# A decoder layer on one core: the next head's first two key projections spread over five places inside the triangular joins

## The chip, the cores and the metric

One core of a Trainium2 chip runs the whole kernel in one launch. Its engines are TensorE (PE; its weight loads are shown apart as PEld), VectorE (DVE), ScalarE (ACT), GpSimd (POOL) and SyncE (SP), which issues the DMAs. Every engine works through its own instructions in order and they meet at semaphores. The metric is the device time of one execution in microseconds (us), the median of several runs.

## The reference

The layer adds three terms to x of shape (4, 512, 512), each on a layer-normalised input: a gated delta-rule attention with 16 heads, a cross attention against a context, and a routed low-rank feed-forward. Only the first is touched here. In short:

```python
qkv = silu(causal_conv4(x @ Wqkv))          # per head: q, k, v of 512 tokens x 128
z   = x @ Wz
q, k = l2norm(q) / sqrt(128), l2norm(k)
for t in range(512):                        # per batch and head, M is 128 x 128
    M = M * exp(g[t])
    M = M + outer(k[t], (v[t] - k[t] @ M) * beta[t])
    o[t] = q[t] @ M
out = rmsnorm(o) * norm_w * silu(z);  x = x + out @ Wout
```

## The kernel before

The 16 heads run one after another. A head treats all 4 batches together, and the 512 tokens of each in 4 chunks (`NC`) of 128. Within a chunk the recurrence is solved in closed form, which needs the inverse of a unit lower triangular 128x128 matrix for each of the 16 (chunk, batch) units. In the order of TensorE's instructions a head consists of these stages:

1. **Decays and Grams** (lines 615 to 648): for each chunk the decay products, the transposes of k, and k times k.
2. **Jobs** (lines 694 to 705): the projections of this head's last queries and of z. One projection job is 12 matmuls of 512 columns (`proj`, line 562): four slices of the contraction, each as hi x hi, lo x hi and hi x lo. A job's result stands in one PSUM bank; ScalarE applies the last tap (`tap`), VectorE the other three (`conv`), ScalarE the silu. Between the jobs stand the transposes of v (line 669) and q (line 659). The transposes of q all use bank 2, and each waits until ScalarE has squared the one before it (`q_squares`, line 1100).
3. **Joins** (lines 787 to 804). Meanwhile GpSimd has inverted the 16x16 diagonal blocks (lines 1783 to 1792) and SyncE has brought them through DRAM into `t32` (line 452). The joins double the inverted blocks from 16 to 32, 64 and 128. Each is a pair of products, y and z, with a PSUM eviction between them (`keep...` on ScalarE, `join...` on VectorE). The matmuls are small: 16x16, 32x32 and 64x64 corners of the array. From 32 on each step comes once for chunks 0 and 1 (group 0) and once for chunks 2 and 3 (group 1). Products of keys and queries (`qk`, line 691) stand between them.
4. **Recursion** over the 4 chunks (lines 807 to 838), full-size matmuls again.

The projections of the next head, 7 jobs of 12 matmuls (`AHEAD`), serve as filling. `ahead(count)` issues the next `count` matmuls of this list:

```python
for m in range(part[0], min(part[0] + count, AHEAD * 3 * ND)):
    job, n = divmod(m, 3 * ND)
    if n == 0:
        job_waits(h + 1, job)
    proj(*JOBS[job], JOB_BANK[job], n, n + 1)
```

Before, the first job (key of batch 0, 12 matmuls) is issued in one piece ahead of the last job of this head, 12 more in four blocks of 7, 2, 2 and 1 in the joins (`JOIN_FILL`), and 60 in the recursion (`FILL`). The last head has no filling. All of TensorE's heads are written out; the other engines loop over the middle ones.

Of the kernel before, what the change touches and what calls it, by code (L numbers as in the profile page):

```python
# [32 lines left out]
ACT = mybir.ActivationFunctionType  # L33
# [6 lines left out]
ND = D // P  # L40
# [20 lines left out]
AHEAD = 7  # L61
JOB_BANK = [{Q_: (0, 3, 0, 3)[b], Z_: 1}.get(kind, job % 2) for job, (kind, b) in enumerate(JOBS)]

FILL = ((0, 6), (9, 9), (9, 9), (9, 9))
JOIN_FILL = (7, 2, 2, 1)
HALVES = 2
EARLY, LATE = slice(0, P // 2), slice(P // 2, P)
FRONT = [slice(2 * j * PAIR, 2 * j * PAIR + PAIR) for j in range(2)]
# [8 lines left out]
def layer(nc, x, ctxT, w_heads, w_ba, conv_w, a_log, dt_bias, norm_w, w_out, wqT, bq, wkT, bk, aT, bwT, wgT, out):  # L77
# [24 lines left out]
    ident = sb("ident", [P, P])  # L102
# [21 lines left out]
    q_sq = sb("q_sq", [P, B, NC])  # L124
# [11 lines left out]
    qT = sb("qT", [P, B, NC, P])  # L136
# [11 lines left out]
    y64 = sb("y64", [P, NC, B, P // 2])  # L148
    y1 = sb("y1", [P, 2, B, P])
    w1 = sb("w1", [P, 2, B, P])  # L150
    vv = sb("vv", [P, B, P])
# [6 lines left out]
    y32 = at(place["gt_0"][0], "y32", [P, NC, B, PAIR])  # L158
# [84 lines left out]
    def grid(i):  # L243

        return bank[i][:, :].rearrange("p (b t) -> p b t", b=B)
# [9 lines left out]
    def ktr_bank(c):  # L255

        return (2, 0, 0, 2)[c]

    sems = {}

    def sem(name):
# [18 lines left out]
    head_vecs, gt_done, decay_mm, decay_done, gam_mm, gam_done = (  # L280
        sem(n) for n in ("head_vecs", "gt_done", "decay_mm", "decay_done", "gam_mm", "gam_done"))
# [3 lines left out]
    qtr_done, qsq_done, qeps_done, vtr_done, nv_done, qk_mm, pT_done, qg_done, kg_done = (  # L285
        sem(n) for n in ("qtr_done", "qsq_done", "qeps_done", "vtr_done", "nv_done", "qk_mm", "pT_done", "qg_done", "kg_done"))
# [83 lines left out]
    with nc.Block() as block:  # L370
# [151 lines left out]
        def _(pe):  # L522
            mm, tr = nc.tensor.matmul, nc.tensor.transpose
# [89 lines left out]
            def head(h, first, more):  # L613

                for c in range(NC):
# [12 lines left out]
                    for b in range(B):  # L628
                        last = tr(grid(ktr_bank(c))[:, b, :], kT[:, b, c, :], ident[:, :])
# [11 lines left out]
                    for b in range(B):  # L641
                        last = mm(grid(5 + 2 * (c % 2))[:, b, :], kT[:, b, c, :], kT[:, b, c, :], start=True, stop=True)
# [7 lines left out]

                def q_transpose(b):
                    pe.wait_ge(silu_done, 12 * h + conv_index(Q_, b) + 1)
                    if b:
                        pe.wait_ge(qsq_done, 4 * h + b)
                    else:
                        pe.wait_ge(ktok_done, 4 * h + 4)
                        pe.wait_ge(ksq_done, 4 * h + 4)
                    for c in range(NC):
                        last = tr(grid(2)[:, c, :], qT[:, b, c, :], ident[:, :])  # L659
                    last.then_inc(qtr_done, 1)  # L660

                def v_transpose(b):
# [11 lines left out]
                def ahead(count):  # L674

                    if not more:
                        return
# [5 lines that stand above are left out]
                    part[0] += count  # L683
# [12 lines left out]
                for job in range(2 * B, NJ):  # L696
                    kind, b = JOBS[job]
                    if job == NJ - 1:
                        ahead(3 * ND)
                        q_transpose(b - 1)  # L700
                    whole_job(h, job)
                    if kind == Z_:
                        v_transpose(b)
                        if b:
                            q_transpose(b if job == NJ - 1 else b - 1)
# [28 lines left out]
                def join32_y(g):  # L734

                    pe.wait_ge(t32_done, 4 * h + 2 * g + 2)
                    if g and not more:
                        pe.wait_ge(y32_done, 2 * h + 1)
                    hold(pe, "pe")
                    for i in range(2):  # L740
                        for b in range(B):
                            for j in range(2):
                                c = 2 * g + i
                                last = mm(small(front_bank(g, j), BACK[j], i, b), nT[FRONT[j], b, c, BACK[j]],
                                          t32[FRONT[j], b, c, FRONT[j]], start=True, stop=True)
                    last.then_inc(y32_mm, 1)

                def join32_z(g):
                    pe.wait_ge(y32_done, 2 * h + g + 1)
                    if g and not more:  # L750
                        pe.wait_ge(z32_done, 2 * h + 1)
                        pe.wait_ge(z32n_done, 2 * h + 1)
                    hold(pe, "pe")
                    for i in range(2):
                        for b in range(B):
                            c = 2 * g + i
                            for j in range(2):
                                mm(small(back_bank(g, j), FRONT[j], i, b), y32[BACK[j], c, b, :], tT[BACK[j], b, c, BACK[j]],
                                   start=True, stop=True)
                            last = mm(small(back_bank(g, 0), BACK[0], i, b), tT[BACK[0], b, c, BACK[0]], y32[BACK[0], c, b, :],  # L760
                                      start=True, stop=True)
                    last.then_inc(z32_mm, 1)

                def join64_y(g):
                    pe.wait_ge(z32n_done, 2 * h + g + 1)
                    if g == 0:
                        pe.wait_ge(pT_done, 4 * h + 4)
                    hold(pe, "pe")
                    for i in range(2):
                        for b in range(B):  # L770
                            c = 2 * g + i
                            last = mm(large(half_bank(g), LATE, i, b), nT[EARLY, b, c, LATE], t32[EARLY, b, c, EARLY],  # L772
                                      start=True, stop=True)
                    last.then_inc(y64_mm, 1)

                def join64_z(g):
                    pe.wait_ge(y64_done, 2 * h + g + 1)
                    pe.wait_ge(z32_done, 2 * h + g + 1)
                    hold(pe, "pe")
                    for i in range(2):  # L780
                        for b in range(B):
                            c = 2 * g + i
                            last = mm(large(half_bank(g), EARLY, i, b), y64[LATE, c, b, :], tT[LATE, b, c, LATE],  # L783
                                      start=True, stop=True)
                    last.then_inc(z64_mm, 1)
# [1 line left out]
                qk(0)  # L787
                qk(1)
                join16_y()
                ahead(JOIN_FILL[0])  # L790
                join16_z()
                qk(2)
                qk(3)
                ahead(JOIN_FILL[1])
                join32_y(0)
                ahead(JOIN_FILL[2])
                join32_y(1)
                join32_z(0)
                ahead(JOIN_FILL[3])
                join32_z(1)  # L800
                join64_y(0)
                join64_y(1)
                join64_z(0)
                join64_z(1)


                for c in range(NC):
# [3 lines left out]
                    else:  # L811
                        pe.wait_ge(s_done, 3 * h + c)
                        pe.wait_ge(kg_done, 3 * h + c)
                        for b in range(B):
                            last = mm(grid(2)[:, b, :], kdT[:, b, c - 1, :], state[:, c % 2, b, :], start=True, stop=True)  # L815
# [4 lines left out]
                    for b in range(B):  # L820
                        last = mm(grid(3)[:, b, :], tT[:, b, c, :], nv[:, b, c, :], start=True, stop=True)  # L821
# [183 lines left out]
        def _(act):  # L1005
            fn = nc.scalar.activation
# [64 lines left out]
            def head(h, more):  # L1071
# [21 lines left out]
                def q_squares(b):  # L1093
                    act.wait_ge(qtr_done, 4 * h + b + 1)
                    if b:
                        act.wait_ge(qsq_done, 4 * h + b)
                    else:
                        act.wait_ge(ksq_done, 4 * h + 4)
                    for c in range(NC):
                        last = fn(vv[:, c, :], grid(2)[:, c, :], ACT.Square, accum_out=q_sq[:, b, c:c + 1])  # L1100
                    last.then_inc(qsq_done, 1)

                def z_silu(b):
# [67 lines left out]
                def keep32_n(g):  # L1171
                    act.wait_ge(z32_mm, 2 * h + g + 1)
                    fn(t32[BACK[0], :, 2 * g:2 * g + 2, FRONT[0]].rearrange("p b c s -> p c b s"),
                       smalls(back_bank(g, 0), BACK[0]), ACT.Copy, scale=-1.0).then_inc(z32n_done, 1)

                def keep64_y(g):
                    act.wait_ge(y64_mm, 2 * h + g + 1)
                    act.wait_ge(z64_mm, 2 * h)
                    fn(y64[LATE, 2 * g:2 * g + 2, :, :], larges(half_bank(g), LATE), ACT.Copy).then_inc(y64_done, 1)
# [15 lines left out]
                keep32_y(1)  # L1195
                keep32_n(0)
                keep32_n(1)
                if more:
                    tap(h + 1, K_, 1)
                keep64_y(0)  # L1200
                keep64_y(1)


                for c in range(NC):
# [701 lines left out]
```

## Time and profile before

| | |
|---|---|
| median of 3 runs | 2014.83 us (2008.29 to 2018.30) |
| the profiled execution | 2019.99 us, of which the span is 2018.3 |
| PE busy in the span | 1908.4 us (95%) |
| DVE, ACT, POOL busy | 1128.2, 933.0, 743.3 us |
| mean granted TensorE clock | 0.962 of full speed |
| 15 heads, from start of head 0 to start of head 15 | 1394.3 us |

A head here runs from its first decay product (line 619) to that of the next head. Where a time is given as "+43.9" it counts from that start. The profiler draws a matmul longer than it keeps the engine, since matmuls are pipelined; what a matmul costs is the distance between the starts of neighbours.

### The profile page before, as it was taken

What the parts mean: (1) busy time and instruction counts of PE and PEld (TensorE: products, weight loads), DVE (VectorE), ACT (ScalarE), POOL (GpSimd) and SP (SyncE); (2) the same over time, 40 slices, a digit from 0 to 9 for tenths busy, and PEclk for the clock granted to TensorE, in tenths of its full rate; (3) what the DMA queues carried; (4) which work ended last, traced back from release to release, by engine and by line L of the source; (5) the groups of instructions that cost most, each with busy time, mean ns of one, the idle gap of its engine ahead of it and who ended that gap; (6) DMA issues with size and microseconds to landing.
All of it is one profiled execution on the core that took longest, in us unless ns stands there. A gap on an engine that the chain in (4) does not pass through costs nothing.

```text
span 2018.3 us, 45513 instructions
## 1 busy us (share of the span) xinstructions
PE 1908.4 (95%) x16962; PEld 1558.9 (77%) x16962; DVE 1128.2 (56%) x2048; ACT 933.0 (46%) x2987; POOL 743.3 (37%) x1143
## 2 busy tenths in 40 slices
PE   6899999999999999999999999999997799999999
PEld 4688888888888888888888788888887565656574
DVE  6656566565657465655657574656564352524333
ACT  2556464646455555646465655546463221213121
POOL 1345363645445353636264544536361000000000
PEclk9899899999989899989999998999897899999999
DMA  3011111201021111112020111111113503121200
GB/s 117 6 33 40 25 37 28 43 22 38 22 42 29 32 40 25 34 25 44 21 43 22 38 30 35 40 24 36 25 30 145 156 21 94 42 84 52 61 23 21
DMA packets 220198, 87.12 MB, mean 43 GB/s; under 512 B 138320, under 2 KB 204240, under 8 KB 219280
## 3 DMA queue, kind: packets, MB, share of 16 engines
q1 hardware_dynamic: 220048, 84.83, 16.6%
q8 instruction: 130, 2.13, 0.4%
q14 instruction: 20, 0.16, 0.0%
HBM read 57.28 MB, written 27.53 MB: 42 GB/s over the span
## 4 chain that ended last, share of the span: by engine, by line
PE 60%; issue 21%; DVE 9%; ACT 5%; POOL 4%; DMA 1%; POOLq 0%; DVEq 0%; SPq 0%; ACTq 0%
PE bank L562 27%; PE bank L871 4%; DVE vT L1383 3%; PE bank L821 3%; PE bank L830 2%; PE bank L783 2%; PE bank L772 2%; PE bank L691 2%; PE bank L815 2%; ACT vv L1084 2%; PE bank L837 1%; PE bank L934 1%; PE bank L952 1%; PE bank L669 1%; PE bank L659 1%
## 5 line engine op out<-in xcount | busy, mean ns | idle before, releaser
L562 PE MATMUL bank<-x_hi,w_hi 128*128 128x512 f32 x1024 | 429.8, 420 | 14.7 <-DVE vT L1383 14.3
L562 PE MATMUL bank<-x_hi,w_lo 128*128 128x512 f32 x1024 | 408.9, 399 | 1.8 <-issue 1.8
L562 PE MATMUL bank<-x_lo,w_hi 128*128 128x512 f32 x1024 | 406.5, 397 | 0.0
L562 PEld LDWEIGHTS bank<-x_hi,w_hi 128*128 128x128 f32 x1024 | 196.0, 191 | 55.6 <-issue 13.4
L562 PEld LDWEIGHTS bank<-x_hi,w_lo 128*128 128x128 f32 x1024 | 195.7, 191 | 45.6 <-issue 2.2
L562 PEld LDWEIGHTS bank<-x_lo,w_hi 128*128 128x128 f32 x1024 | 196.6, 192 | 32.0 <-issue 0.6
L1383 DVE SCALAR_TENSOR_TENSOR qT<-bank,cw,qT 128x511 f32<-128x511 f32 (+2 forms) x192 | 142.1, 747 | 51.0 <-ACT qT L1033 46.5
L1848 POOL TENSOR_TENSOR rstd<-ve,mhalf 128x1 f32<-128x1 f32 x32 | 17.4, 544 | 390.2 <-DVE ve L1607 390.2
L1216 ACT ACTIVATE o_tmp<-bank 128x128 f32<-128x128 f32 x256 | 67.4, 278 | 179.0 <-PE bank L837 179.0
L1383 DVE SCALAR_TENSOR_TENSOR vT<-bank,cw,vT 128x511 f32<-128x511 f32 (+2 forms) x192 | 143.0, 745 | 8.6 <-ACT vT L1033 4.1
L1383 DVE SCALAR_TENSOR_TENSOR kT<-bank,cw,kT 128x511 f32<-128x511 f32 (+2 forms) x192 | 143.4, 747 | 5.0
L1816 POOL TENSOR_TENSOR o_rstd<-o_ms,minus_half 128x4 f32<-128x4 f32 x64 | 70.5, 1101 | 200.4 <-DVE o_ms L1525 200.4
L1805 POOL TENSOR_TENSOR qT<-qT,gam 128x512 f32<-128x512 f32 x48 | 59.9, 1275 | 182.0 <-PE bank L691 182.0
L1821 POOL TENSOR_TENSOR state<-state,gam 128x512 f32<-128x512 f32 x32 | 33.6, 1051 | 209.0 <-PE bank L837 204.7
L871 PE MATMUL bank<-wo_hi,o_hi 128*128 128x512 f32 x256 | 105.4, 412 | 0.0
L871 PE MATMUL bank<-wo_hi,o_lo 128*128 128x512 f32 x256 | 100.0, 391 | 0.0
L871 PE MATMUL bank<-wo_lo,o_hi 128*128 128x512 f32 x256 | 100.0, 391 | 0.0
L1484 DVE STREAM_TRANSPOSE tT<-t 128x512 f32<-128x512 f32 x64 | 39.9, 680 | 98.3 <-DMA t<-blkT_d 98.3
L837 PE MATMUL bank<-w,pT 128*128 128x128 f32 x512 | 92.0, 277 | 0.0
L1210 ACT ACTIVATE w<-bank 128x512 f32<-128x512 f32 x64 | 38.3, 598 | 111.1 <-PE bank L821 111.1
L1118 ACT ACTIVATE nv<-bank,k_norm 128x128 f32<-128x128 f32 x256 | 72.9, 374 | 33.0 <-PE bank L669 33.0
L1788 POOL TENSOR_TENSOR prod<-blkN,blkT 128x15 f32<-128x15 f32 (+7 forms) x240 | 65.9, 275 | 54.2 <-DMA blkN<-blkN_d 36.7
(221 smaller groups left out, 4447.3 us busy)
## 6 DMA issues: line engine op xcount, KB each, us to landing
w_raw<-in_w_heads SPq DMA_DIRECT2D x64, 256.0 KB, 2.8
o_d<-og SPq DMA_DIRECT2D x64, 256.0 KB, 2.6
o_raw<-o_d SPq DMA_DIRECT2D x16, 1024.0 KB, 6.2
x_in<-in_x SPq DMA_DIRECT2D x16, 256.0 KB, 3.6
blkN_d<-nT SPq DMA_DIRECT2D x64, 64.0 KB, 2.0
t<-blkT_d SPq DMA_DIRECT2D x64, 64.0 KB, 2.4
wo_raw<-in_w_out SPq DMA_DIRECT2D x4, 1024.0 KB, 9.5
x_res<-in_x SPq DMA_DIRECT2D x16, 256.0 KB, 2.8
```

Source lines behind the costliest of these rows:

```text
L562: last = mm(bank[bk][:, :], w[:, kind % 2, d, :], xx[:, d, b * S:(b + 1) * S], start=(n == 0), stop=(n == 3 * ND - 1))
L691: last = mm(grid(5 + 2 * (c % 2))[:, b, :], kT[:, b, c, :], qT[:, b, c, :], start=True, stop=True)
L772: last = mm(large(half_bank(g), LATE, i, b), nT[EARLY, b, c, LATE], t32[EARLY, b, c, EARLY], start=True, stop=True)
L821: last = mm(grid(3)[:, b, :], tT[:, b, c, :], nv[:, b, c, :], start=True, stop=True)
L837: last = mm(grid(4)[:, b, :], pT[:, b, c, :], w1[:, c % 2, b, :], start=(c == 0), stop=True)
L871: last = mm(bank[c % 2][:, :], o[:, c % 2, k, :], w[:, k, :], start=(n == 0), stop=(n == 3 * H - 1))
L1118: last = fn(nv[:, b, c, :], grid(6)[:, c, :], ACT.Copy, scale=k_norm[:, b, c:c + 1])
L1216: last = fn(o_tmp[:, b, :], grid(4)[:, b, :], ACT.Square, accum_out=o_sq[:, c, b:b + 1])
L1383: stt(d[:, k:S], bank[JOB_BANK[JOBS.index((kind, b))]][:, 0:S - k], cw[:, kind, TAPS - 1 - k:TAPS - k], d[:, k:S], ALU.mult, ALU.add).then ...
L1788: tt(products, blkN[:, j, j + 1:BLK].unsqueeze(2).to_broadcast([P, below, j + 1]), blkT[:, j, 0:j + 1].unsqueeze(1).to_broadcast([P, below ...
L1805: tt(qT[:, :, c, :], qT[:, :, c, :], gam[:, :, c, :], ALU.mult).then_inc(qg_done, 1)
L1816: tt(o_rstd[:, c, :], o_ms[:, c, :], minus_half[:, 0:B], ALU.pow).then_inc(orstd_done, 1)
```

## The change

The first key job is no longer issued in one piece ahead of the last job of the head. Its 12 matmuls and the 12 that were in the joins before (the second key job) now stand in the joins in five blocks: 8 before the z product of the 16-join, 5 before y of the 32-join, 5 before z of it, 3 before y of the 64-join and 3 before z of it. In the 32-join the two groups' y steps now follow each other directly, and so do their z steps. The transposes of q alternate between bank 2 and bank 4, so each waits for the squares of the one before the last. ScalarE's tap of the second key job moves behind the two evictions of the 64-join's y.

```diff
-JOIN_FILL = (7, 2, 2, 1)
+JOIN_FILL = {"z16": 8, "y32": 5, "z32": 5, "y64": 3, "z64": 3}
...
+    def qtr_bank(b):
+        return (2, 4)[b % 2]
...
                 def q_transpose(b):
                     pe.wait_ge(silu_done, 12 * h + conv_index(Q_, b) + 1)
-                    if b:
-                        pe.wait_ge(qsq_done, 4 * h + b)
+                    if b >= 2:
+                        pe.wait_ge(qsq_done, 4 * h + b - 1)
+                    elif b:
+                        pe.wait_ge(gam_done, 4 * h + 4)
...
                     if job == NJ - 1:
-                        ahead(3 * ND)
                         q_transpose(b - 1)
                     whole_job(h, job)
...
                 join16_y()
-                ahead(JOIN_FILL[0])
+                ahead(JOIN_FILL["z16"])
                 join16_z()
                 qk(2)
                 qk(3)
-                ahead(JOIN_FILL[1])
+                ahead(JOIN_FILL["y32"])
                 join32_y(0)
-                ahead(JOIN_FILL[2])
                 join32_y(1)
+                ahead(JOIN_FILL["z32"])
                 join32_z(0)
-                ahead(JOIN_FILL[3])
                 join32_z(1)
+                ahead(JOIN_FILL["y64"])
                 join64_y(0)
                 join64_y(1)
+                ahead(JOIN_FILL["z64"])
                 join64_z(0)
                 join64_z(1)
...
                 keep32_n(1)
+                keep64_y(0)
+                keep64_y(1)
                 if more:
                     tap(h + 1, K_, 1)
-                keep64_y(0)
-                keep64_y(1)
```

## Rows read from the trace of the kernel before

**Rows 1.** The page: span, and busy time of each engine.

```profile
span 2018.3 us, 45513 instructions
...
PE 1908.4 (95%) x16962; PEld 1558.9 (77%) x16962; DVE 1128.2 (56%) x2048; ACT 933.0 (46%) x2987; POOL 743.3 (37%) x1143
```

**Rows 2.** Windows, one per head: start:end, length, busy times, PEclk, DMA; heads 1, 2, 8, sum.

```profile
170.20:265.50 95.30, 92.36 (x956) 80.26 (x954) 56.82 (x97) 51.23 (x175) 44.78 (x68) 0.95 0.15 32
265.50:354.40 88.90, 87.65 (x955) 76.00 (x954) 56.67 (x96) 51.24 (x175) 44.92 (x68) 1.00 0.15 34
...
822.60:917.20 94.60, 91.51 (x954) 78.78 (x953) 56.71 (x97) 51.24 (x175) 44.81 (x68) 0.95 0.14 32
...
sum 1394.30, PE 1356.51 PEld 1176.62 DVE 850.93 ACT 768.48 POOL 671.20; mean PE 90.43 PEld 78.44 DVE 56.73 ACT 51.23 POOL 44.75
```

**Rows 3.** TensorE's waits in heads 0 to 14 together: total, times, longest.

```profile
PE bank L730 <- issue: 7.5, 13, 2.3
...
PE bank L758 <- issue: 5.2, 5, 1.4
PE bank L719 <- ACT vv L1100: 3.7, 15, 0.3
PE bank L691 <- issue: 3.7, 3, 1.8
...
PE bank L760 <- issue: 2.3, 2, 1.3
PE bank L562 <- issue: 1.8, 1, 1.8
PE bank L772 <- issue: 1.6, 2, 1.0
```

**Rows 4.** Windows late in the joins and behind them, head 1, then head 2.

```profile
224.20:227.60 3.40, 2.12 (x66) 1.69 (x66) 1.58 (x4) 1.45 (x4) 0.84 (x1) 1.00 0.00 0
227.60:237.90 10.30, 10.30 (x71) 9.60 (x70) 4.29 (x7) 2.00 (x4) 0.52 (x1) 0.50 0.09 28
...
319.50:322.90 3.40, 3.40 (x91) 3.36 (x82) 2.92 (x6) 2.25 (x4) 0.69 (x2) 1.00 0.02 5
322.90:333.20 10.30, 10.26 (x77) 9.21 (x76) 6.88 (x13) 3.55 (x12) 2.06 (x2) 1.00 0.11 27
```

**Rows 5.** The page's DMA queue that carries instructions.

```profile
q8 instruction: 130, 2.13, 0.4%
```

**Rows 6.** TensorE's timeline in head 10 (start, us, what, count, idle before).

```profile
1045.21 0.47 PE L562 MATMUL bank<-x_hi,w_hi 128*128 128x512 f32 x1
...
1048.04 0.60 PE L659 MATMUL bank<-ident,qT 128*128 128x128 f32 x4
...
1054.32 1.25 PE L719 MATMUL bank<-t,nT 16*32 16x16 f32 x128 [0.24 <-ACT vv L1100]
1055.50 0.50 PE L562 MATMUL bank<-x_hi,w_hi 128*128 128x512 f32 x1
...
1057.33 0.89 PE L730 MATMUL bank<-tT,y 32*16 32x16 f32 x88
...
1060.91 0.47 PE L562 MATMUL bank<-x_lo,w_hi 128*128 128x512 f32 x1
...
1061.58 0.69 PE L744 MATMUL bank<-t,nT 32*32 32x32 f32 x32
```

**Rows 7.** VectorE's timeline in head 10, first transpose of the joins.

```profile
1051.61 2.49 DVE L1484 STREAM_TRANSPOSE tT<-t 128x512 f32<-128x512 f32 x4 [5.56 <-DMA t<-blkT_d]
```

**Rows 8.** The page: the same transposes in all heads.

```profile
L1484 DVE STREAM_TRANSPOSE tT<-t 128x512 f32<-128x512 f32 x64 | 39.9, 680 | 98.3 <-DMA t<-blkT_d 98.3
```

**Rows 9.** ScalarE's timeline in head 10: v for the last batch; tap of key 0, evictions of the 32-join.

```profile
1051.89 1.14 ACT L1118 ACTIVATE nv<-bank,k_norm 128x128 f32<-128x128 f32 x4 [2.07 <-PE bank L669]
...
1061.46 0.69 ACT L1033 ACTIVATE kT<-bank,cw 128x512 f32<-128x512 f32 x1 [1.45 <-PE bank L691]
1062.31 0.77 ACT L1168 ACTIVATE y<-bank 32x256 f32<-32x256 f32 x2 [0.16 <-PE bank L744]
```

**Rows 10.** TensorE's waits over the whole span: the query transposes.

```profile
PE bank L659 <- ACT vv L1100: 2.0, 1, 2.0
```

More of the change, by code:

```diff
@@ L64 @@
 FILL = ((0, 6), (9, 9), (9, 9), (9, 9))
-JOIN_FILL = (7, 2, 2, 1)
+JOIN_FILL = {"z16": 8, "y32": 5, "z32": 5, "y64": 3, "z64": 3}
+assert sum(JOIN_FILL.values()) + sum(sum(f) for f in FILL) == AHEAD * 3 * ND
 HALVES = 2
@@ L658, in q_transpose @@
                     for c in range(NC):
-                        last = tr(grid(2)[:, c, :], qT[:, b, c, :], ident[:, :])
+                        last = tr(grid(qtr_bank(b))[:, c, :], qT[:, b, c, :], ident[:, :])
                     last.then_inc(qtr_done, 1)
@@ L1099, in q_squares @@
                     for c in range(NC):
-                        last = fn(vv[:, c, :], grid(2)[:, c, :], ACT.Square, accum_out=q_sq[:, b, c:c + 1])
+                        last = fn(vv[:, c, :], grid(qtr_bank(b))[:, c, :], ACT.Square, accum_out=q_sq[:, b, c:c + 1])
                     last.then_inc(qsq_done, 1)
```

## The prediction

> **What bounds the kernel now.** I read the page first, for its busy shares: TensorE is busy for 1908.4 of 2018.3 us, the next engine for 56% of the span [rows 1]. So the kernel is as long as TensorE's stream, and a change that only reorders this stream can gain in two places: where TensorE waits, and where its clock is low. The windows by head come next. The 15 heads that a next head follows take 1394.3 us together, 93.0 each, but they differ: five of them, head 2 the shortest, have a granted clock of 1.00 and take 88.9 to 91.2 us; ten have 0.93 to 0.98 and take 92.8 to 95.7 us, heads 1 and 8 among them [rows 2]. Their work is the same. The difference is what can be had.
>
> The waits of TensorE in these heads show the second thing: the large ones are put down to "issue", to no other engine, and they stand before the small matmuls and just behind them (lines 730, 758, 760, 772, also 691 and 562) [rows 3]. Their sum is 7.5 + 5.2 + 3.7 + 2.3 + 1.8 + 1.6 = 22.1 us. I take them to be instruction fetch: the queue that carries instructions brought 130 packets and 2.13 MB [rows 5], that is 16 KB each, and TensorE's 2 x 16962 instructions [rows 1] over 130 are 261 for each packet. A step of the 16-join issues 128 weight loads and 128 matmuls in 1.18 us (1055.50 less 1054.32) [rows 6], a whole packet's worth, and 8 matmuls of a projection take longer than that with 16 instructions.
>
> The third view is a pair of stretches late in the joins. In head 1 TensorE is busy for 2.12 of 3.40 us there (a wait of 1.2 us in line 758 lies in it), and the next 10.30 us run at a granted clock of 0.50, 1.2 instead of 2.4 GHz. In head 2, without that wait, it is busy throughout and the clock stays at 1.00 [rows 4]. The waits in lines 758, 760 and 772 are nine in nine heads, 9.1 us together [rows 3]; eight of these nine heads are among the ten with a lower clock. The other two, heads 8 and 13, have a wait of 1.8 (line 562) or 2.3 us (line 730) earlier in the joins [rows 3], and their clock falls there. So one late wait of about 1 us in a stretch with little dense work is followed by a fall that costs more than the wait.
>
> **The price of a fall.** The eight heads with a late wait and a lower clock take 94.7 us on average (head 1: 95.30), head 2 takes 88.90 [rows 2]. Of the 5.8 between them 1.55 are their own issue waits (for head 1: 1.2 + 0.7). So a fall costs 4.2 us. Half of the 10.3 us at the low clock [rows 4] would be 5.1, a check from above.
>
> **The change part by part.** Reordering moves 12 projection matmuls; none is added.
>
> *What leaves the jobs stage.* The block of 12 goes from 1045.21 to 1048.04 [rows 6], 2.83 us; I allow 0.08 for two query transposes that now touch, so what follows comes 2.75 us earlier. The first 16-join product, at 1054.32 after a wait of 0.24, would be reached at 1051.33.
>
> *What it meets there.* That step needs `t32`. VectorE, which waits for the same DMA, starts at 1051.61 in head 10 after 5.56 us of idling [rows 7]; over 16 heads it idles 98.3 us [rows 8], 6.14 each, so on average the data are there 0.6 us later than in head 10, at 1052.2. GpSimd and SyncE bring them from the Grams on, which the change does not touch. The squares of the last queries are no later: ScalarE's v step begins at 1051.89 and the join 2.43 behind it [rows 9, 6]; both come 2.75 earlier, at 1051.6, provided the alternate banks let the other transposes pass. They do: the third transpose now waits only for the squares of the first, and the second projection block before it gives ScalarE the time. So the join starts at 1052.2 instead of 1054.32, only 2.1 us earlier, and 0.6 to 0.9 us of TensorE's time turn into a wait for the DMA. This is the new cost: the cover is gone.
>
> *What enters the joins.* A block of 7 took 1.83 us (1055.50 to 1057.33), a block of 2 took 0.67 (1060.91 to 1061.58) [rows 6]: 0.23 for each matmul and about 0.21 for each block. Twelve more matmuls and one block more are 2.76 + 0.21 = 2.97, less some 0.12 because the last block of one cost more than this: 2.85. The net without any change in waits or clock is 2.85 - 2.1 = +0.75 us per head, +11 us over 15 heads.
>
> *Evictions behind blocks.* ScalarE's tap of key 0 takes 0.69 and now stands before the 32-join's evictions with less time in hand, since key 0 is complete only with the fourth matmul of the block before y32. The two groups' evictions take 0.77 each [rows 9], some 2.2 us with the tap; TensorE has the end of that block, two y steps of 0.6 and a block of 5 (1.36) to spend. They fit with some 0.2 us to spare for group 0, so nothing. VectorE's convolution of key 0 still ends before the 64-join's z. The tap of key 1, moved back, is used only in the recursion. Their cost is nothing while the covers hold; with a late y eviction it would be up to 0.5 us in a head.
>
> *Issue waits.* The z step of the 16-join has one projection matmul more before it, so the 13 waits in line 730 shrink by about 0.2 each. The late waits stood behind 920 instructions issued in 10 us from the start of the joins; (counted in the code); now some 930 are spread over 11 us, so of about 1 us each half should remain. 13 x 0.2 + 9 x 0.45 = 6.5 us saved. Bounds: 0, and 22.1.
>
> The Trainium skill, on its page "Runtime: NRT & Kernel Launch", section "Instruction fetch mechanics", says that instructions come in blocks of 16 KiB, 256 of them, and that this is hidden because dispatch is slower than the fetch. The trace agrees on the block, 2.13 MB over 130 packets, and does not bear out that it is hidden, since its 22.1 us of waits lie where 256 instructions pass in 1.18 us. By the page's rule this term would be 0 and the sum 6.5 us higher.
>
> *The clock.* After the change every stretch of the late joins holds dense blocks: 5, 3 and 3 matmuls between the steps where before there were 2 and 1. I expect the eight late falls to end, less one that stays or appears elsewhere: -7 x 4.2 = -30 us. Bounds: 0, and all ten, -40.
>
> *The last head* has no filling. Its third query transpose waits 2.0 us for the squares now [rows 10] and no longer will; the DMA limits that gain to about 1 us.
>
> Sum: +11 - 6.5 - 30 - 1 = -26.5 us. The profiled execution took 2019.99 us, 5.2 above the median of 2014.83; it would go to 1993.5, and I carry the difference over to the median: **1988.3 us**, 1.3% less.
>
> **The rivals.**
> - *The clock falls as before* because the small steps decide, not what stands between them. For it: the steps themselves are left as they are. Against it: head 2's late joins have only one dense block in them and stay at 1.00. Time: +11 - 6.5 - 1 = +3.5, 2018 us, within 0.5%.
> - *Half of the falls stay*: -26.5 + 15, 2003 us.
> - *Slower: the new wait brings the fall forward.* In front of the first 16-join product there are now 0.85 us without work and then 1.2 us of tiny matmuls. Should the clock fall there, the dense blocks behind it run at half speed, as in head 8, whose fall is that early: 94.60 us [rows 2]. Ten heads have falls now, so it decides once more than ten do. All 15 at 94.6 + 0.75 are 1430 us, +36 us: 2051 us. Twelve such heads and three at 89.7 are 1413: +19, or 2034 us. Against it: before that wait stand full-size matmuls without a gap, behind the tiny step 2 us of dense ones; with a wait of 0.24 no fall came there unless an issue wait of 1.8 us was added.
> - *Everything falls into place*: all ten falls gone, the late issue waits too, the DMA wait at its shortest (head 10): +7 - 11 - 40 - 2 = -46, 1969 us.
>
> **How the numbers follow.** The forecast's case, -15 to -38 us, has 0.50; everything in place 0.15; half of the falls 0.14; as before 0.13; slower 0.08. A measurement of this kernel can tell about 0.5%, 10 us, from no change. Half of the falls is on the faster side, but near the bound, so a part of it counts as same: faster 0.75, same 0.17, slower 0.08. The likeliest case's own range is 1977 to 2000. The range for 8 in 10 takes in the lower bounds and half of the falls and some of the case as before: 1966 to 2011.
>
> **What would show it.** In the profile after: the windows by head with a granted clock of 1.00 in nearly all of them and lengths of 89 to 91.5 us. Line 719's counterpart waits some 0.7 us, put down to the DMA into `t32` or to VectorE, not 0.24 for ScalarE. Waits by "issue" before lines 758, 760 and 772 fall from 9.1 to about 5 us or less. PE's busy time falls with the clock by some 30 us or more, since it counts slow matmuls as busy. The prediction is wrong if clocks of 0.5 stay in the joins of many heads, or if the waits for the evictions of the 32-join appear.

## The result and the profile after

| | before | after |
|---|---|---|
| median | 2013.53 us (4 runs, 2008.29 to 2018.30) | 1984.66 us (4 runs, 1982.82 to 1993.02) |
| profiled execution, its span | 2019.99, 2018.3 us | 1982.82, 1980.8 us |
| heads 0 to 14 | 1394.3 us | 1362.4 us |

The ratio after/before is 0.9865, with a 95% interval from 0.9827 to 0.9904: 1.35% faster. Forecast were 1988.3 us and 1.3%. The two profiled executions lie 37.2 us apart, the medians 28.9: the one before is slower than all four timed runs, the one after is the fastest of its four. What follows is read from these two, so its terms add up to more than the medians differ by. The page after, answering to [rows 1]; DVE, ACT and POOL have the work they had:

```profile
span 1980.8 us, 45513 instructions
...
PE 1878.9 (95%) x16962; PEld 1529.2 (77%) x16962; DVE 1128.5 (57%) x2048; ACT 930.1 (47%) x2987; POOL 741.5 (37%) x1143
```

The windows by head, answering to [rows 2]; the columns are as there, and the number behind POOL's count is the granted clock. Heads 1, 3, 4, 13 and the sum:

```profile
169.90:258.90 89.00, 87.72 (x956) 75.98 (x954) 56.77 (x97) 51.05 (x175) 44.80 (x68) 1.00 0.16 34
...
352.80:444.50 91.70, 89.31 (x953) 77.00 (x953) 56.72 (x96) 51.05 (x175) 44.70 (x68) 0.98 0.15 33
444.50:533.30 88.80, 87.65 (x955) 75.85 (x954) 56.82 (x97) 51.06 (x175) 44.71 (x68) 1.00 0.15 34
...
1256.70:1352.30 95.60, 91.38 (x955) 78.81 (x954) 56.81 (x96) 51.04 (x175) 44.70 (x68) 0.95 0.14 31
...
sum 1362.40, PE 1329.47 PEld 1147.83 DVE 851.60 ACT 765.75 POOL 669.55; mean PE 88.63 PEld 76.52 DVE 56.77 ACT 51.05 POOL 44.64
```

Eight heads now have a granted clock of 1.00, where five had. The other seven have 0.95 to 0.98, and what is low in them is mostly short: the low stretches of the 15 heads add up to 34.1 us, where they were 92.2. The shortest head, 88.8 us, is no shorter than head 2 was [rows 2]: an undisturbed head costs what it did, and the gain is in the disturbed ones.

TensorE's waits in these 15 heads, answering to [rows 3] (725 is the first product of the 16-join, 719 before; 736 its z, 730 before; 698 the queries' products; 567 the projections):

```profile
PE bank L725 <- DMA t<-blkT_d: 11.9, 15, 1.9
...
PE bank L725 <- issue: 4.7, 2, 2.5
...
PE bank L736 <- issue: 2.2, 6, 0.6
PE bank L698 <- issue: 2.0, 2, 1.5
PE bank L567 <- issue: 1.9, 1, 1.9
```

The issue waits fell from 22.1 to 4.7 + 2.2 + 2.0 + 1.9 = 10.8 us, and those late in the joins, nine of them with 9.1 us before, are gone from this execution (a second profile of the same kernel, below, has four short ones, 1.1 us together). New is the wait for the DMA, 0.79 us per head.

The timeline of TensorE in head 4, a head without an issue wait, answering to [rows 6] (start, us, what):

```profile
485.85 1.25 PE L725 MATMUL bank<-t,nT 16*32 16x16 f32 x128 [0.45 <-DMA t<-blkT_d]
487.03 0.50 PE L567 MATMUL bank<-x_hi,w_hi 128*128 128x512 f32 x1
...
489.07 1.22 PE L736 MATMUL bank<-tT,y 32*16 32x16 f32 x128
...
493.37 1.21 PE L750 MATMUL bank<-t,nT 32*32 32x32 f32 x64
...
502.82 1.16 PE L828 MATMUL bank<-nv,tT 128*128 128x128 f32 x8
```

The block of 8 takes 2.04 us (487.03 to 489.07). From the first product of the joins to the first of the recursion (line 828) it is 16.97 us. The first product stands at +41.3 in this head; it was at +43.9.

The falls that are left lie elsewhere. Windows of head 3, around the 16-join:

```profile
392.00:396.40 4.40, 2.69 (x139) 2.53 (x141) 1.15 (x2) 2.12 (x12) 2.27 (x2) 1.00 0.58 123
396.40:399.80 3.40, 3.40 (x32) 2.65 (x20) 2.51 (x5) 2.41 (x8) 0.00 (x0) 0.50 0.00 0
399.80:404.20 4.40, 4.40 (x151) 3.76 (x149) 2.75 (x6) 0.75 (x2) 0.81 (x1) 1.00 0.02 4
```

Here TensorE waited 1.71 us for the DMA and then ran the 128 tiny products. The clock was at 1.2 GHz for the next 3.4 us, and back at 2.4 GHz behind the block of 8. So it is in six of the seven heads, between +43.6 and +54.5; in head 8 it follows a wait of 1.5 us at line 698, from +48.5 on. Heads 0, 3 and 10 are those with the longest waits for the DMA (1.86, 1.71 and 0.98 us); heads 2, 5 and 13 have an issue wait of 1.9 to 2.5 us at this place. None of heads 0 to 14 has a low clock from the 32-join to the end of the recursion. Head 15, which has no filling, runs at 1.2 GHz from +43.9 to +71.2, through its joins.

### The profile page after: what moved, and what is told of

Same layout as the page of the kernel before. It is cut to its first block, busy times and chain, and to the rows that moved or that the text cites. A ratio compares the mean times of both kernels' runs of the same rounds, so it can differ in the third digit from the quotient of the medians.

```text
span 1980.8 us, 45513 instructions
## 1 busy us (share of the span) xinstructions
PE 1878.9 (95%) x16962; PEld 1529.2 (77%) x16962; DVE 1128.5 (57%) x2048; ACT 930.1 (47%) x2987; POOL 741.5 (37%) x1143
## 4 chain that ended last, share of the span: by engine, by line
PE 44%; issue 25%; POOL 13%; DVE 6%; DMA 5%; ACT 4%; SPq 2%; POOLq 1%; DVEq 0%; ACTq 0%
PE bank L567 14%; PE bank L878 4%; POOL blkT L1799 3%; POOL prod L1795 3%; PE bank L828 2%; POOL k_tok L1765 2%; PE bank L837 2%; DMA blkT_d<-blkT 2%; PE bank L698 2%; DVE vT L1390 2%; DMA t<-blkT_d 2%; PE bank L778 2%; ACT vv L1091 2%; PE bank L789 2%; PE bank L822 2%
## 5 line engine op out<-in xcount | busy, mean ns | idle before, releaser
L1760 POOL TENSOR_TENSOR pT<-pT,cvec 128x512 f32<-128x512 f32 x64 | 67.1, 1049 | 46.3 <-DVE cvec L1461 46.3
L1365 DVE TENSOR_TENSOR w_lo<-w_raw,w_hi 128x512 fp32r<-128x512 f32 x64 | 44.6, 697 | 68.4 <-ACT w_hi L1029 68.4
```

Source lines behind the costliest of these rows:

```text
L1365: tt(w_lo[:, kind % 2, :, :], w_raw[:, kind % 2, :, :], w_hi[:, kind % 2, :, :].bitcast(F32), ALU.subtract).then_inc(wlo_done, 1)
L1760: tt(pT[:, :, c, :], pT[:, :, c, :], spread(cvec[:, :, c]), ALU.mult).then_inc(lc_done, 1)
```

## The experiments

Ratios are to runs of the kernel before on the same chip, with 95% intervals. "Late" is said of waits for issue before the 32-join's z and the 64-join's steps, and of falls that begin between the 32-join's y and the start of the recursion, in heads 0 to 14.

**Grouping alone.** The kernel before, both groups' steps together:

```diff
                 join32_y(0)
-                ahead(JOIN_FILL[2])
                 join32_y(1)
+                ahead(JOIN_FILL[2] + JOIN_FILL[3])
                 join32_z(0)
-                ahead(JOIN_FILL[3])
```

> The kernel before with one part of the change alone: both groups' 32-join y steps follow each other, and so do the z steps, with the fill of 12 in blocks of 7, 2 and 3. Theory (the gain is the clock, kept up by dense blocks between the late steps, plus shorter instruction waits): little dense work is added late, so falls late in the joins stay in at least five heads and the time is within 8 us of before, 2006 to 2020. Rival (fewer changes between small and large matmuls give the gain): one block less per head is some 0.2 us, and if the order itself ended the late waits the time would be 1990 or less.

Measured: 2010.75 us, ratio 1.0005 (0.9987 to 1.0023), no change. Late waits stay at 6.8 us (9.1 before):

```profile
PE bank L758 <- issue: 4.0, 5, 1.2
...
PE bank L760 <- issue: 2.4, 3, 1.1
```

Eight heads have a late fall, as before. The grouping is not where the gain is.

**The banks alone.** The kernel before with `qtr_bank` and its waits, and nothing else.

> The kernel before with one part of the change alone: the query transposes alternate between banks 2 and 4; the block of 12 stays ahead of the third transpose. Theory (with the block there the squares are done in time, so there is nothing to save but one wait in the last head): 2.0 us less at most in the last head, time as before within 4 us. Rival (the alternation itself brings the first 16-join product forward): 2000 us or less.

Measured: 2007.31 us, ratio 0.9969 (0.9940 to 0.9999). The interval allows from nothing to 0.6%, 12 us; the profile still has late falls in eight heads, so there is no sign that the alternation does more by itself.

**The banks undone.** The changed kernel with all query transposes in bank 2:

```diff
-        return (2, 4)[b % 2]
+        return 2
...
-                    if b >= 2:
-                        pe.wait_ge(qsq_done, 4 * h + b - 1)
-                    elif b:
-                        pe.wait_ge(gam_done, 4 * h + 4)
+                    if b:
+                        pe.wait_ge(qsq_done, 4 * h + b)
```

> The changed kernel with all query transposes in bank 2 again, each waiting for the squares of the one before. Theory: the third transpose follows the second directly and waits for its squares, some 1.9 us of TensorE in each head, of which the wait for the DMA before the first 16-join product gives back 0.7: +1.2 us x 15 = +18 us against the changed kernel, about 2003 us. Rival: the wait for the DMA covers all of it, 1985 us.

Measured: 2017.66 us, ratio 1.0027 (1.0005 to 1.0050): the whole gain is gone, by the ratios 33 us and more than the 18 expected. The profiled execution, 2010.4 us, is among the quickest of its ten. Its waits:

```profile
PE bank L664 <- ACT vv L1105: 29.5, 15, 2.0
...
PE bank L723 <- ACT vv L1105: 3.5, 15, 0.2
```

The third transpose waits 1.97 us in each head. Nothing of that is given back, since the joins then again begin behind ScalarE's squares (0.2 us each) and not behind the DMA, which is ready by then; I had counted on 0.7. Seven of the heads also have a fall next to that wait, from +37 or +38 on. No head has a late fall, and there is no late wait either.

**Dense work moved to the end of the joins, and away from it.** Two kernels, the changed one with other fills, the same 24 matmuls:

```diff
-JOIN_FILL = {"z16": 8, "y32": 5, "z32": 5, "y64": 3, "z64": 3}
+JOIN_FILL = {"z16": 14, "y32": 5, "z32": 5, "y64": 0, "z64": 0}    # first
+JOIN_FILL = {"z16": 8, "y32": 4, "z32": 2, "y64": 5, "z64": 5}     # second
```

> The changed kernel with the same 24 matmuls in the joins, but 14, 5, 5, 0, 0 instead of 8, 5, 5, 3, 3: the 64-join has no dense blocks. Theory (dense work in the late joins keeps the clock up): low clock returns late in the joins or the start of the recursion in several heads, at about 4 us each; with the falls at the first 16-join product kept, 2000 to 2020 us. Rival (all the gain is from spacing instructions, and the longer block of 14 spaces the 16-join better still): no fall late in the joins, 1975 to 1985 us.

> The changed kernel with the same 24 matmuls, shifted to the end: 8, 4, 2, 5, 5, so 14 instead of 18 stand before the 64-join. First theory of the prediction (dense blocks beside the 64-join keep the clock there): no late fall, about 1985 us. Theory after the first runs (a late wait, that is, 0.9 us less between the first fetch and the 64-join, brings the fall, and dense work behind it does not prevent it): issue waits late in the joins return in four or more heads, falls in three or more, 1992 to 2008 us.

Measured: without dense work beside the 64-join 1979.19 us, ratio 0.9847 (0.9830 to 0.9863), so at least as good as the change, and the rival's time; with ten matmuls there instead of six, and fewer before, 2007.21 us, ratio 0.9969 (0.9933 to 1.0006), nearly the whole gain lost. The waits of the first:

```profile
PE bank L764 <- issue: 1.7, 2, 1.5
...
PE bank L766 <- issue: 0.4, 2, 0.3
```

and of the second:

```profile
PE bank L764 <- issue: 5.3, 4, 1.8
...
PE bank L766 <- issue: 2.1, 2, 1.5
```

The first has late falls in two heads, 1 and 9, both of which have one of these waits (1.5 and 0.3 us). The second has them in three, 6, 9 and 14, beside waits of 1.4 to 1.8 us; head 3 waits 1.6 us without one. They last 13.7 to 17.1 us, where the eight before lasted 6.8 to 13.7. The profiled execution is one of the slower ones, 2017.1 us where the ten runs go from 1993.9 to 2020.2. Head 6, windows:

```profile
681.00:685.40 4.40, 2.94 (x136) 2.38 (x132) 2.25 (x5) 2.17 (x7) 2.34 (x2) 1.00 0.02 4
685.40:702.50 17.10, 17.10 (x94) 14.44 (x94) 5.00 (x9) 2.71 (x5) 0.52 (x1) 0.50 0.05 17
```

The blocks of 5 lie in these 17.1 us at 1.2 GHz. Dense work behind the wait did not keep the clock; it ran at half speed. This kernel has fewer matmuls before the wait and more behind it, so it does not say by itself which of the two matters; the next one adds them behind only.

**Dense work added to the kernel before.** Six matmuls into a bank that is free at that point, in two threes:

```diff
+                def repeat(count):
+
+                    if more:
+                        for i in range(count):
+                            mm(bank[3][:, :], w_hi[:, 0, 0, :], x_hi[:, 0, 0:S], start=(i == 0), stop=(i == count - 1))
...
+                repeat(3)
                 join64_y(0)
                 join64_y(1)
+                repeat(3)
                 join64_z(0)
```

> The kernel before with six dense matmuls of 512 columns added, which nothing uses: three before the 64-join's y steps and three before its z steps; the rest, the block of 12 ahead of the last job and the query transposes, as before. Added work 6 x 0.23 + 0.3 = 1.7 us per head, +25 us. Theory (dense work late in the joins ends the late falls at 4.2 us each, and the pause shortens the waits before the 64-join): -30 us against it, so 2003 to 2012, no slower than before although work is added. Rival (clock falls depend on the waits alone, which lie before the added work): 2030 us or more.

Measured: 2053.66 us, ratio 1.0189 (1.0123 to 1.0255), 41 us more where the added work is 25 us. I had expected no slower. Late falls stay in six heads, each beside a late wait of 0.9 to 1.8 us, and last 13.7 us in five of them and 17.1 in one. In head 3 a fall that begins earlier, at +47.5 with an issue wait of 1.1 us and another of 1.5 us behind it, lasts 27.3 us. Dense work behind the wait neither keeps the clock nor ends the fall.

**The fill kept where it was.** The block of 12 stays ahead of the last job, and the 12 in the joins are spread as 4, 3, 2, 2, 1:

> The changed kernel with the block of 12 left ahead of the last job, where it was before, and the 12 matmuls that were in the joins spread over the same five places as 4, 3, 2, 2, 1. Theory (the added dense work and time in the joins separate the small steps and keep the clock): half of it is missing, the wait after the first 16-join step grows by about 0.7 us, and late waits and some late falls return: 2000 to 2012 us. Rival (spreading over five places is what counts, and the uncovered wait for the DMA costs): 1985 us or less.

Measured: 2023.67 us, ratio 1.0050 (1.0020 to 1.0079), slower than before and than expected. The block of 4 no longer covers ScalarE's eviction of y (line 737), and the late waits are back:

```profile
PE bank L737 <- ACT y L1160: 8.4, 14, 0.6
PE bank L737 <- issue: 7.9, 13, 2.3
...
PE bank L765 <- issue: 3.1, 3, 1.2
```

Late falls are in four heads, and nine falls begin before the 32-join's y. So the 12 moved matmuls are needed; spreading alone does harm.

**Are the issue waits instruction fetch?** The changed kernel a second time, and once with 128 semaphore instructions added on TensorE before head 0:

```diff
+            for _ in range(128):
+                hold(pe, "pe")
             for h in range(H):
```

> The changed kernel once more, unaltered, for a second profile. Theory (issue waits are instruction fetch, whose block boundaries lie at fixed instructions of the program): the waits of over 1 us stand in the same heads and at the same steps as in the first profile, after the 16-join's y in heads 2, 5 and 13 and at the queries' products in head 8, each within 0.5 us. Rival (chance in the memory system): other heads.

> The changed kernel with 128 semaphore instructions added once, on TensorE, ahead of head 0, half a fetched block of 256; some 1 to 6 us of added work. Theory (fetch): every later block boundary lies 128 instructions earlier in the work, so heads 2, 5, 8 and 13 lose their waits of over 1 us and others get them. Rival (something at these places or times of the heads): the same heads keep them.

Measured, one run each: 1982.45 us and 2014.81 us. In the second profile of the same kernel the four heads 2, 5, 8 and 13 have the long waits again. In head 8 they agree to the hundredth, the first profile and then the second:

```profile
853.88 1.44 PE L698 MATMUL bank<-qT,kT 128*128 128x128 f32 x6 [1.54 <-issue]
```

```profile
851.84 1.44 PE L698 MATMUL bank<-qT,kT 128*128 128x128 f32 x6 [1.54 <-issue]
```

Head 5 has 1.93 and 2.02 us in the block behind y. In heads 2 and 13 it moved by one step, from y to z of the 16-join (2.20 to 2.06 and 2.50 to 2.06 us), where I had expected the same step; in both the DMA wait before was over 0.7 us longer. The DMA waits themselves differ from run to run, head by head. With 128 instructions before them, heads 2, 8 and 13 have no issue wait of 1 us or more, heads 1, 4, 9 and 12 have, and head 5's is at the 32-join's z. So a wait hangs on where in the program an instruction stands. With packets of 16 KB [rows 5] this is what the fetch of instructions would do. The times of the packets on queue q8 say the same: in the traces of the kernel before, the changed one and the shifted one, all 37 issue waits over 0.4 us inside heads 0 to 14 end 2.3 to 3.0 us after a packet has started there, though such moments make up only 15 to 17% of the time in the joins (taken as +44 to +60). Two packets never start less than 3.2 us apart. The shifted kernel took as long as the kernel before. Of the 32.4 us between the two executions 16.4 lie ahead of head 0, 11.3 in heads 0 to 14 (1374.0 in place of 1362.7 us, two of them with late waits of 0.9 and 1.7), and the rest behind. So the gain may hang in part on this position; with one execution of each, and 10 us between the fastest and slowest run of the changed kernel, that is not shown. My price for the added instructions was wrong: TensorE stood for 14.5 us, not 1 to 6, before head 0.

**Filling the new wait.** Three of the 24 matmuls in front of the first product:

```diff
+JOIN_FILL = {"y16": 3, "z16": 8, "y32": 5, "z32": 4, "y64": 2, "z64": 2}
...
+                ahead(JOIN_FILL["y16"])
                 join16_y()
```

> The changed kernel with three of the 24 matmuls moved in front of the first 16-join product, into the wait for the DMA: 3, 8, 5, 4, 2, 2. Theory: the wait of 0.36 to 1.9 us before that product (0.8 on average) is filled with 0.7 us of work that leaves the later joins, and dense work next to the tiny step ends some of the falls there: -0.5 us x 15 from the wait and -1.5 us in each of about four heads, 1970 to 1978 us. Rival (falls there come from the tiny matmuls and the instruction waits behind them, and two matmuls less in the 64-join let late falls return): 1985 us or more.

Measured: 1982.16 us, ratio 0.9867 (0.9848 to 0.9886), not to be told from the change, and above the 1970 to 1978 expected. The DMA wait halved to 5.5 us, but with one matmul less in the block before the 32-join's z a late wait of 1.7 us came back in one head, with its fall, and five falls at the 16-join stayed.

**Splitting the 16-join** by blocks in the middle of y and of z (2, 4, 5, 4, then 2, 3, 2, 2):

> The changed kernel with the 24 matmuls spread to separate the instructions of the 16-join: 2 before its y, 4 in the middle of its y, 5 before its z, 4 in the middle of its z, then 2, 3, 2, 2. Theory (waits by issue are instruction fetch, longest where 128 matmuls of 16 columns pass at once, and falls follow such waits of over 1 us): the waits over 1 us in heads 2, 5, 8 and 13 become shorter than 1 us, most falls there end; three or four more changes between small and large matmuls cost 0.7 us per head: 1968 to 1980 us. Rival (less dense work behind the 16-join brings the late waits back): 1990 us or more.

Measured: 2032.36 us, ratio 1.0109 (1.0078 to 1.0140). The rival held: the waits in heads 5 and 13 became two of 1.2 to 1.3 us each, and neither head has a fall, but the late waits returned, with late falls in six heads, and TensorE now waits for VectorE's transposes before the 32-join as well:

```profile
PE bank L754 <- DVE t L1508: 5.9, 13, 0.5
...
PE bank L768 <- issue: 5.2, 6, 1.3
...
PE bank L770 <- issue: 3.7, 3, 1.6
```

**The best version.** All of the fill before the 64-join, three of it before the first product:

```diff
+JOIN_FILL = {"y16": 3, "z16": 9, "y32": 5, "z32": 7, "y64": 0, "z64": 0}
```

> The changed kernel with the 24 matmuls as 3 (before the 16-join's y), 9, 5, 7, 0, 0. Theory (late waits come before the 64-join and are ended by time before it; after it dense work does nothing): no wait over 1 us and no fall late in the joins, the wait for the DMA filled, two blocks fewer in the 64-join: 1970 to 1978 us, fastest of all but the split one. Rival (the 64-join without dense work loses the clock): 1990 us or more.

Measured: 1967.76 us (1965.40 to 1968.76), ratio 0.9766 (0.9722 to 0.9809), the fastest, and faster than the 1970 to 1978 expected. The intervals of this and of the change do not overlap. Its 15 heads:

```profile
sum 1347.50, PE 1314.93 PEld 1142.38 DVE 848.74 ACT 765.80 POOL 670.26; mean PE 87.66 PEld 76.16 DVE 56.58 ACT 51.05 POOL 44.68
```

and its waits (829 is the first product of the recursion):

```profile
PE bank L725 <- DMA t<-blkT_d: 6.8, 10, 1.3
...
PE bank L698 <- issue: 4.7, 3, 2.2
PE bank L829 <- DVE tT L1517: 4.5, 13, 0.4
PE bank L736 <- issue: 4.5, 4, 1.8
...
PE bank L764 <- issue: 0.3, 1, 0.3
```

One late wait of 0.3 us, no late fall, and three falls behind the 16-join, in heads 2, 5 and 8. The DMA wait is 6.8 us. The price is VectorE's last eviction, uncovered without a block before the 64-join's z: 4.5 us.

**All kernels in one table.** Ordered by the number of large matmuls between the 16-join's z and the last of the 32-join's z steps; waits and falls of heads 0 to 14 in the profiled execution of each. The small steps between the two places are the same in all.

| large matmuls there | kernels | late issue waits, us | heads with a late fall |
|---|---|---|---|
| 5 | before, grouping, banks alone, dense work added, 12 kept, split | 9.1, 6.8, 7.6, 7.8, 5.1, 9.2 | 8, 8, 8, 6, 4, 6 |
| 6 | moved to the end | 7.6 | 3 |
| 9 | three before the first product | 2.0 | 1 |
| 10 | the change, again, shifted, one bank, moved away | 0, 1.1, 3.2, 0, 2.4 | 0, 0, 1, 0, 2 |
| 12 | best | 0.3 | 0 |

The split kernel decides what is counted: it has all 24 matmuls in the joins and 20 of them before the 64-join, more than the change, but only 5 between the two steps, and its late waits are as large as those of the kernel before. The kernels differ in more than this number, so the table shows an order and proves no cause.

## Why the prediction came out right, and where its steps were off

The time was right, and so were the two places of the gain, waits for issue and the clock. The terms, in the profiled executions (-37.5 us of span; forecast -26.5, while the medians moved by -28.9):

- *Undisturbed head*: forecast +0.75 us each, +11. Measured: head 2 before, 88.9 less its 0.2 of issue wait, against head 4 after, 88.8 plus 0.34 because its DMA wait was 0.45 and the average is 0.79: +0.4 each, some +6. The new wait was placed and sized right (0.6 to 0.9 forecast, now named after the DMA). The joins grew from 14.57 us (head 2 before, +43.88 to +58.45) to 16.97, by 2.4 and not by 2.85, in these two heads.
- *Issue waits*: forecast -6.5, measured -11.3. The late ones did not halve, they went in this execution. The forecast set some 930 instructions against 920; by the counts of the code that is what lies before the 64-join, while before the first late wait, in line 758, there were about 730.
- *The clock*: forecast -30, that is seven of eight late falls gone and one new. What remains of -31.9 us for the 15 heads is -31.9 + 11.3 - 6 = -27. The low stretches shrank by 58 us, and half of that, 29, is the most that a clock of one half can have cost, so the two agree. All eight late falls went. Of the seven low stretches after, six lie right behind the first 16-join step, the place the slower rival named. The rival was right about the place and wrong about the price. It took head 8 of before, 10.2 us of low clock, for each; five of the seven low stretches after are 3.4 us long. Head 3 after, 2.9 us longer than head 4, had 1.3 of this from its DMA wait, so such a fall costs about 1.6, not 4.2.
- *Last head and the rest*: forecast -1, measured -5.6 (before head 0 -1.2, from head 15 on -4.4). The transpose's wait of 2.0 us is gone and the joins begin at +41.2 instead of +43.2, so it gave 2.0 and not 1. The rest was not separated from the clock's course.

By its own signs the forecast held in part. PE's busy time fell by 29.5 us, and the wait for the DMA came as described. But the granted clock is 1.00 in eight heads and not in nearly all, and a clock of 0.5 stays in the joins of seven of the 15, which was named as a sign of being wrong. These stretches lie earlier, and five of the seven are shorter than any late one before. That the clock term is so close (-27 for -30) is in part luck: the reason given for it did not hold.

**The step that failed** is the reason given for the clock: "after the change every stretch of the late joins holds dense blocks". The blocks beside the 64-join do nothing for it. Without them late falls stay away in 13 of 15 heads and in the best version in all; with more of them at the cost of the earlier ones the falls return and last longer; added to the kernel before they only cost. What the change does is put more large matmuls, and so time, between the 16-join's z and the 32-join's z: with 9 or more there the late waits are 0 to 3.2 us in all and at most two heads have a late fall, with 5 or 6 they are 5.1 to 9.2 us and three to eight heads have one. That a late wait is what brings the fall is seen in all profiles as a pairing (nearly every late fall has a late wait, though some of only 0.2 to 0.4 us and one none, and waits of 1.6 and 1.7 us stand in heads without a fall); a kernel in which the wait alone is taken away was not made, so the link is strong but not shown by itself.

The alternating banks are what lets the block leave: by themselves they give at most 0.6%, and without them the change is no faster than the kernel before. The prediction had them as a condition, unpriced; the price is 28 us between the profiled executions and 33 by the ratios.

The Trainium skill, page "Runtime: NRT & Kernel Launch", section "Instruction fetch mechanics", has the fetch hidden behind slower dispatch. That is not borne out here: the waits moved with 128 instructions of displacement, and they end 2.3 to 3.0 us after a packet has started on the queue that carries instructions.

## What to carry to other kernels

A stream of very small matmuls can outrun its instructions: look for waits by "issue" behind them and for a low granted clock behind these waits, and put ordinary work between the steps that run through the instructions and the place of the wait, not ahead of both and not behind. When work is moved away from a place, ask what it covered there; here a DMA that came out as 0.8 us of waiting per head. Three matmuls in front of it halved that wait, without a measurable gain of their own. And where the waits fall depends on the position of the instructions in the program, so measure several arrangements of the same fill rather than one.

## What the runs showed of the hardware that was not expected

- The same 24 matmuls in the same five or six places, differently divided, gave 1967.8 to 2007.2 us, ratios of 0.9766 to 0.9969.
- 128 semaphore increments on TensorE took 14.5 us, 0.11 us each, against 256 instructions of a 16-join step in 1.18 us.
- The falls were longer with more dense work behind the late wait: 13.7 to 17.1 us with six matmuls added or ten instead of six there, 6.8 to 13.7 us in the kernel before, 6.8 us in both heads of the kernel with its 24 moved away from the 64-join. The one late fall of the shifted kernel, with six beside the 64-join, lasted 10.2 us.
